# Local attention of a two-layer block: the weighing of the values in four tiles of 32 columns instead of two of 64

## What is computed

```python
h = shift_token(x)
q, k, v = split(h @ wqkv)                 # 8 heads of 64
q, k = l2norm(q) * qs, l2norm(k) * ksc
q, k = rotary_xpos(q, k)
# windows of 128 tokens; each query sees its own window and the one before
sim = einsum('bhwid,bhwjd->bhwij', q * 8, look_around(k))
attn = softmax(where(mask, -max, sim))
o = einsum('bhwij,bhwjd->bhwid', attn, look_around(v))
x = x + o @ wo                            # wo: 512 x 256
```

## Time and profile before

| | |
|---|---|
| median of 3 runs | 4812.37 us (4810.68 to 4820.48) |
| the profiled execution | 4814.37 us, its span 4812.7 us |
| busy, whole span | PE 4133.8 us (86%), DVE 3551.4 (74%), ACT 2512.8 (52%), POOL 1192.9 (25%) |
| local attention, layer 0 | from about 888.5 to 1419.0 us |
| local attention, layer 1 | from about 1658.0 to 2187.5 us |

### The profile page before, as it was taken

How to read it: one execution, slowest core, us unless ns; L and a number is a source line. 1 busy time by engine, 2 the same in 40 slices (tenths; PEclk the granted TensorE clock), 3 DMA queues, 4 the chain that set the end, 5 groups by cost and what they waited for, 6 DMA issues and landing times. The chain is left out here.

```text
span 4812.7 us, 92751 instructions
## 1 busy us (share of the span) xinstructions
PE 4133.8 (86%) x36572; PEld 2378.7 (49%) x36572; DVE 3551.4 (74%) x5543; ACT 2512.8 (52%) x3342; POOL 1192.9 (25%) x878
## 2 busy tenths in 40 slices
PE   7999999298869878896966999999999999736995
PEld 4788888155545445564643323232333333424664
DVE  4677777688865488885576889999988887465544
ACT  2566666244434344443312567687888777302552
POOL 1000000677741167751042000000000000311554
PEclk9999999699989889998977899999999999756998
DMA  1000000222220022221026000000000000102443
GB/s 56 1 1 1 1 1 1 60 48 49 48 41 19 4 52 48 48 40 38 0 69 124 13 4 11 10 3 4 9 4 10 4 12 6 59 18 92 102 99 93
DMA packets 289241, 156.68 MB, mean 33 GB/s; under 512 B 214368, under 2 KB 280884, under 8 KB 288820
## 3 DMA queue, kind: packets, MB, share of 16 engines
q1 hardware_dynamic: 250276, 100.68, 10.2%
q0 software_dynamic: 13440, 20.98, 2.4%
q10 hardware_dynamic: 25136, 29.64, 1.9%
HBM read 72.72 MB, written 33.55 MB: 22 GB/s over the span
## 5 line engine op out<-in xcount | busy, mean ns | idle before, releaser
L1972 DVE TENSOR_REDUCE s_tops<-ps 128x2 f32<-128x1024 f32 (+3 forms) x1152 | 1261.2, 1132 | 197.2 <-PE ps L1862 139.3
L1941 ACT ACTIVATE s_weights<-ps 128x1024 f32<-128x1024 f32 (+3 forms) x1152 | 1093.4, 952 | 394.6 <-PE ps L1874 204.7
L1893 PE MATMUL ps<-s_weights,v_flat 128*32 128x256 f32 (+1 forms) x8704 | 692.8, 391 | 6.4 <-ACT s_o_t L1947 5.6
L1858 PE MATMUL ps<-keys,s_q 48*128 48x512 f16 (+3 forms) x2304 | 437.9, 377 | 45.5 <-DMA s_q<-qk_parts 21.5
L1874 PE MATMUL ps<-s_q,keys 50*128 50x512 f16 (+3 forms) x2304 | 435.1, 374 | 30.7 <-DVE s_tops L1972 14.1
L428 PE MATMUL ps<-a_qt,a_kt 128*128 128x256 f16 x3072 | 375.4, 273 | 3.8 <-POOL s_ones L412 3.8
L2008 POOL CAST s_shift<-s_minus_top 128x16 f16<-128x16 f32 x32 | 6.3, 196 | 1491.4 <-DVE s_minus_top L1979 1491.4
L994 ACT ACTIVATE w_all<-ps 128x1024 f32<-128x1024 f32 x124 | 127.2, 1026 | 454.7 <-PE ps L905 454.7
L915 PE MATMUL ps<-la_wqkv,la_yt 128*128 128x512 f16 x1152 | 286.9, 397 | 88.8 <-DMA la_yt<-la_y_parts 81.4
L1874 PEld LDWEIGHTS ps<-s_q,keys 50*128 50x128 f16 x2304 | 112.3, 93 | 495.0 <-issue 286.9
L428 PEld LDWEIGHTS ps<-a_qt,a_kt 128*128 128x128 f16 x3072 | 300.7, 98 | 40.4 <-POOL s_ones L412 4.2
(11 more groups left out here) (338 smaller groups left out, 7664.2 us busy)
## 6 DMA issues: line engine op xcount, KB each, us to landing
ex_w_whole<-in_L_ffn_w_dram ACTq DMA_DIRECT2D x16, 1024.0 KB, 7.1
qk_parts<-a_parts SPq DMA_DIRECT2D x64, 128.0 KB, 2.4
keys<-qk_parts SPq DMA_DIRECT2D x48, 128.0 KB, 5.8
s_q<-qk_parts SPq DMA_DIRECT2D x48, 128.0 KB, 4.5
w_all<-in_L_ffn_wqkv_dram SPq DMA_DIRECT2D x3, 1536.0 KB, 6.4
x<-in_x_dram SPq DMA_DIRECT2D x4, 1024.0 KB, 9.1
a_table<-in_rope_dram POOLq DMA_DIRECT2D x8, 512.0 KB, 5.6
heads_out<-s_o_now SPq DMA_DIRECT2D x32, 128.0 KB, 1.9
```

What stands on the lines that cost most here:

```text
L1858: mm = pe.matmul(m.ps[:, bank, 0:width], b.q[rows(half, KEY_PARTS * L1_DH), place % 2, pair, t * P:(t + 1) * P], m.keys[rows(half, KEY_PAR ...
L1893: mm = pe.matmul(m.ps[h * QUAD:(h + 1) * QUAD, OUT, begin:end], m.v_flat[:, first:first + QUAD], weights[:, a % 2, h, begin:end], start=(k ...
L1941: act.activation(weights[:, a % 2, 2 * pair:2 * pair + 2, skip:CHUNK], m.ps[:, bank:end + 1, skip:CHUNK], ACT.Exp).then_inc(s["exp"], 1)
L1972: dve.tensor_reduce(tops[:, u % 2, :, i % 2, t, c], m.ps[:, bank:end + 1, 0:width], AX.X, ALU.max).then_inc(s["max"], 1)
```

## The change

`weigh` uses four tiles of 32 columns, one for each of the four heads of a round, so that head (h, g) has rows 32 x (2h + g) and following of the bank. The 64 features of a head are made in two parts of 32, each in 128 columns of its own, and the totals are a third part. A round has 24 matmuls of 128 moving columns. Totals stand in 128 columns, and the product reads them twice by a broadcast. The output weights are loaded by eight DMAs in the new order of features.

```diff
 def load_attention(eng, m, f, layer, loaded):
 ...
-    eng.dma_start(m.wo, layer_of(f["wo"], layer).rearrange("o (k p) e -> p (o k) e", p=P)).then_inc(loaded, 16)
+    wo = layer_of(f["wo"], layer).rearrange("o (r g h d l) e -> (o r) g h l d e", r=2, g=2, h=2, d=2)
+    for r in range(2):
+        for h in range(2):
+            for g in range(2):
+                at = (2 * h + g) * QUARTER
+                eng.dma_start(m.wo[at:at + QUARTER, 2 * r:2 * r + 2, :], wo[r, g, h, :, :, :]).then_inc(loaded, 16)
 ...
-ATTENTION_LOADS = 4
+ATTENTION_LOADS = 11
 ...
-        ones = sb("ones", [P, DH])
+        ones = sb("ones", [P, QUARTER])
 ...
-        rtotal = sb("rtotal", [P, 2 * P])
+        rtotal = sb("rtotal", [P, P])
 ...
-                    for g in range(2):
-                        for kind in range(2):
-                            at = kind * 2 * P + g * P
-                            for i, (key, b) in enumerate(blocks):
-                                for h in range(2):
-                                    col = (2 * (2 * r + g) + h) * DH
-                                    by = ones[:, :] if kind else v[:, key % SLOTS, col:col + DH]
-                                    mm = pe.matmul(m.ps[rows(h), OUT, at:at + P], by, weights[:, key % 2, r, h, g, b, :],
-                                                   start=(i == 0), stop=(i == len(blocks) - 1), skip_group_check=True)
+                    for part in range(3):
+                        for i, (key, b) in enumerate(blocks):
+                            for h in range(2):
+                                for g in range(2):
+                                    to = (2 * h + g) * QUARTER
+                                    col = (2 * (2 * r + g) + h) * DH + part * QUARTER
+                                    by = ones[:, :] if part == 2 else v[:, key % SLOTS, col:col + QUARTER]
+                                    mm = pe.matmul(m.ps[to:to + QUARTER, OUT, part * P:(part + 1) * P], by, weights[:, key % 2, r, h, g, b, :],
+                                                   start=(i == 0), stop=(i == len(blocks) - 1), tile_position=(0, to), skip_group_check=True)
 ...
-                    dve.reciprocal(rtotal[:, :], m.ps[:, OUT, 2 * P:4 * P]).then_inc(s["recip"], 1)
+                    dve.reciprocal(rtotal[:, :], m.ps[:, OUT, 2 * P:3 * P]).then_inc(s["recip"], 1)
                     dve.wait_ge(s["recip"], ROUNDS * w + r + 1)
-                    dve.tensor_tensor(o[:, r, :], m.ps[:, OUT, 0:2 * P], rtotal[:, :], ALU.mult).then_inc(s["o"], 1)
+                    dve.tensor_tensor(o[:, r, :].rearrange("p (d q) -> p d q", d=2), m.ps[:, OUT, 0:2 * P].rearrange("p (d q) -> p d q", d=2),
+                                      rtotal[:, :].unsqueeze(1).broadcast_to([P, 2, P]), ALU.mult).then_inc(s["o"], 1)
```

More of the change, by code:

```diff
@@ L574, in _ @@
                     halves(b)
+QUARTER = P // 4
 def load_attention(eng, m, f, layer, loaded):
     eng.dma_start(m.wqkv, layer_of(f["wqkv"], layer).rearrange("o (k p) e -> p (o k) e", p=P)).then_inc(loaded, 16)
-    eng.dma_start(m.wo, layer_of(f["wo"], layer).rearrange("o (k p) e -> p (o k) e", p=P)).then_inc(loaded, 16)
+    wo = layer_of(f["wo"], layer).rearrange("o (r g h d l) e -> (o r) g h l d e", r=2, g=2, h=2, d=2)
[4 more added lines that the diff above has]
+                eng.dma_start(m.wo[at:at + QUARTER, 2 * r:2 * r + 2, :], wo[r, g, h, :, :, :]).then_inc(loaded, 16)
     for n, name in enumerate(("q_scale", "k_scale")):
```

## The result

The changed kernel takes **4735.59 us** (median of 4 runs, 4727.55 to 4740.69) where the kernel before took 4812.47 beside it, a ratio of 0.9836 with a 95% interval of 0.9818 to 0.9853. It is faster by 77 us; the forecast was 116, with 4736 inside the range. The profiled execution took 4736.55 us, its span 4734.9.

A forecast was written before the change was run, and what follows sets the result against it. Circles of waits between engines, not one engine, bound the local attention's windows. Savings of 97.2 us in 54 full windows and 19.2 at the layers' ends, together 116.4 off 4812.4, gave 4696 us; range 4680 to 4745.

The forecast's parts named there:

- Circle A: Chain of waits through DVE, ACT, POOL and PE in a full window: two reciprocals, one weighing; 14.91 us, forecast 12.88.
- C: Circle not in the prediction: find and scores (PE), exponentials and queries_for_before (ACT), high_o, low_o, rotate, reciprocal, product, weigh; 13.30 us.
- Weighing: PE's weighing round in local attention: twelve slots of four abreast records, 1.31 us for 1.75, 0.44 saved.
- Rival 2: PE's weighing: four tiles don't keep abreast over twelve slots, 0.87 us more a round, 4829 us; chance 0.06.
- rival 4: Whole kernel: all the gain is eaten elsewhere, 4812 us; chance 0.03.
- Loads: Output-weight loads on SP: seven more DMA issues, hidden under other work; priced at nothing, at most 3.2 us.
- Full windows: The 54 full windows of local attention, both layers: each saves 1.80 us, 97.2 us together.
- B bounds at 13.12: Full windows: the runner-up circle (rotate, reciprocal, sums, POOL's norms, normalise, low_o), one reciprocal, falls from 13.92 and bounds.
- Ends of the layers: Last stretch of each layer's local attention, where DVE and PE wait in turn: 9.6 us saved a layer, 19.2 together.
- reciprocals and weighings add up: Last stretch of each layer: savings of both operations sum, 1.68 us for each of three steps between windows.
- Rival 1: Full windows: a third circle through the queries' transposes binds, landings 1.0 us later, 1.17 a window, 4730 us; chance 0.20.
- Rival 3: Full windows: a wait in POOL's runner-up circle (power or tables) goes too, so Circle A bounds, 4683 us; chance 0.09.

## Why the prediction was right, and where its size was off

- **What bounds.** Right in kind: circles of waits, not an engine, with `rotate` still waiting for POOL's tables and `weigh(i, 1)` for the product. The search for circles was too short. Circle A was followed from the release that the timeline names; nobody asked of each step what stands ahead of it in its own engine's order. Before, ACT idled 0.26 us ahead of `high_o`. With the 0.10 by which neighbouring ACT rows overlap (1869.33 + 1.14 less 1870.37 above), the slack of C was 0.36. C holds one reciprocal and one weighing, A two reciprocals and one weighing, so A shrinks by 0.80 more than C, and 0.80 is more than 0.36. C is then 14.91 - 0.36 - 0.80 - 0.46 = 13.29, as measured.
- **Reciprocal.** Taken 0.95 us, measured 951 ns. **Product.** 0.42 as taken. **Weighing.** Taken 1.31 for twelve slots, 0.44 saved; a round went from 1.91 to 1.45, 0.46 saved. The estimate by the Trainium skill's ratio of 2.38 (TensorE: Matmul & The Clock Gate, Measured speedup vs the span model) would have left 1.81 to the next operation; the trace disagrees, four tiles ran fully abreast for twelve slots. Rival 2 is out, and so is rival 4.
- **Loads.** Nothing, as taken.
- **Full windows.** 97.2 forecast, 71.6 measured (403.55 + 403.38 less 368.81 + 366.54). The step "B bounds at 13.12" failed: C held 13.29, so 54 x (14.91 - 13.29) = 87.5. The long windows took 17.7 - 1.8 = 15.9 of that; the sum had put nothing for them.
- **Ends of the layers.** 19.2 forecast, 12.4 measured in this profile (56.23 + 56.24 less 49.21 + 50.81), of which 1.3 is one `project_o` that happened to run at the higher clock. The step "reciprocals and weighings add up" held from round 0 to round 1: 4.37 became 3.14. It failed from window to window, where another chain took over: the shift, from DVE over SP's transpose and copy back to PE. The timeline of the last windows, after:

```profile
1347.77 0.92 DVE L1086 TENSOR_SCALAR la_shift<-la_top 128x8 bf16<-128x8 f32 x1
...
1351.00 1.62 SPq L788 DMA_DIRECT2D band<-la_shift_t  x2
...
1354.26 0.60 PE L909 MATMUL ps<-band,spread 128*128 128x256 bf16 x4 [1.14 <-issue]
...
1359.73 0.96 DVE L1118 RECIPROCAL la_rtotal<-ps 128x128 f32<-128x128 f32 x1 [5.14 <-PE ps L954]
```

  PE stands 1.14 us at L909, and the reciprocal behind it waits 5.14 us instead of 3.59. The row names no releaser, but the last update of the copies' semaphore is at 1354.16, 0.09 us before PE starts, so the 1.14 are the shift's; no run took them away. The shortfall itself repeats: the ends of the layers took 50.1 and 51.2 us in the changed kernel run again, where the forecast had 46.6.
- **Rival 1** (query transposes late) named a real loss and was wrong in form: not every window 1 us longer, but 9 of 54, on top of another bound, and the larger stops in the middle of a layer are those for the shift rows, which it did not have. It needed landings 0.4 us later, and 4.7 for 3.2 was there in the trace of before. It belonged in the sum, at its frequency, not beside it.
- **Rival 3** did not come true in the changed kernel, where `tables` still takes 1.51 us. Its mechanism is real all the same: with `high_o` first, that row fell to 0.46 and B below 13.12.
- **Luck.** The forecast of 4696 is 40 us too low. The time lies in the range because the range was stretched for rival 1, and 4736 is near rival 1's 4730 by chance: some 10 us of the gap are circle C's, 16 the long windows' (of which the query transposes have a part), 7 the ends of the layers'.
- **Elsewhere.** Both attentions lose 83.7 us (530.33 and 528.86 to 488.30 and 487.21), the profiled executions differ by 77.8. The rest is in unchanged stages: what follows the second attention took 2624.67 us before and 2631.87 after, and between 2620 and 2634 over the runs of these experiments.

## What to carry to other kernels

When a circle of waits is shortened, list for each of its instructions both who releases it and what its engine does just before: the gap between them is the slack of the next circle, and the smallest gap says how much of the gain survives. Transfers with a rare late landing are priced by how often they land late times what is then missing, once the work after them moves closer. Column tiles paid here only with neighbouring matmuls in different tiles, and most of their gain was on another engine: totals in half the columns for the reciprocal.

## What was not expected of the hardware

- A POOL row of `tables` took 1.51 us beside DVE's `low` (1858.87 and 1858.86 in the changed kernel) and 0.46 where `low` came after it. Of two such rows the one that starts later was the longer one: `low` took 1.39 us for 1.22 when a row of `tables` was ahead of it (996.66 and 996.80). A row's time is set by its neighbour, so a sum of rows along a circle holds only while the rows keep their neighbours. The Trainium skill (Advanced Engine Details and Errata, GPSIMD Details) says that POOL shares a read and a write interface with DVE and conflicts with its instructions that read two inputs from SBUF, as `low` does; the trace agrees, and these runs put the price at 1.05 us for this row.
- Taking work off PE alone cost the clock: an idle stretch grown from 1.51 to 1.97 us before each second weighing, granted clock 1.00 to 0.95 over the full windows, no time gained; 12 repeated matmuls a window, with the stretch at 0.66 us, brought 23 us back.
- The query transposes that landed over 3.5 us after their issue (8 of 28 in the changed kernel, 4 of 27 before) each had a packet of the instruction queue between 0.55 us before and 1.2 us after their issue; the one above had it 1.04 us after. Of those in time, 1 of 20 and 2 of 23 had one. With `score(i, 1)` early, all 9 late ones had it too, up to 1.74 us after. That is a coincidence in the trace; no run changed the instruction packets, so the cause is not shown.
